# A macaron layer on one core: the second routing in two parts, rows 0 to 2 inside the last attention and row 3 inside the second FFNs

## The reference

```
x = x + 0.5 * ffn(layernorm(x))        # first FFN
x = x + attention(layernorm(x))
x = x + 0.5 * ffn(layernorm(x))        # second FFN

ffn(x):  logits = x.reshape(b, 512*512) @ switch_w.T + switch_b      # 8 experts, 8 MB of weights
         gate, idx = top_k(softmax(logits), 2)                       # per row of the batch
         o = sum over the 2 experts of gate * (gelu(xh @ w1 + b1) @ w2 + b2)   # heads of 32 features
         return (x + o) @ w3.T + b3
attention(x): q, k, v, a, g = x @ w_in.T;  q normed per head, k = tanh(k), a = clip(sigmoid(a+2))
         mem = recurrence of k*v with decay a over the tokens (chunks of 64)
         y = g*(q*mem) + (1-g)*v;  return y @ w_out.T
```

## Time and profile before

| | |
|---|---|
| median of 3 runs | 538.1 us |
| profiled execution: time, span | 537.86 us, 536.1 us |
| PE, PEld, DVE, ACT, POOL busy | 91%, 66%, 78%, 40%, 19% of the span |
| mean granted TensorE clock | 0.967 |
| read from HBM, written | 39.34 MB, 8.39 MB |
| attention of row 3 | about 351 to 407 us |
| output tiles of row 3 | 407 to 418 us |
| second routing, its choice | 418 to 431 us, 431 to 442 us |
| second FFNs of rows 1 to 3 with the W tiles of rows 0 to 3 | 456.7 to 536.1 us |

### The profile page before, as it was taken

The page is one execution under the profiler, slowest core; times in us unless marked ns, Lnnn a source line. Parts: engine busy times, 40 slices in busy tenths (PEclk is TensorE's granted clock), DMA queues, the critical chain, the costliest instruction groups (busy, mean ns, idle before and its releaser), DMA issues.

```text
span 536.1 us, 8572 instructions
## 1 busy us (share of the span) xinstructions
PE 487.3 (91%) x3184; PEld 353.8 (66%) x3204; DVE 416.6 (78%) x801; ACT 217.1 (40%) x348; POOL 103.3 (19%) x112
## 2 busy tenths in 40 slices
PE   0556999998999999999999999999999848999997
PEld 0544676666687666768766676866667725777775
DVE  3868888999776599887559988758997779878642
ACT  0226653523724222471412247242244338665640
POOL 5140036000002700001350000145111320021220
PEclk9796999999999999999999999999999968999999
DMA  8999020000102000010200001033665060131112
GB/s 338 409 376 409 3 78 2 1 1 0 40 20 74 26 1 0 2 40 21 98 0 0 0 0 39 20 137 135 240 226 223 4 208 31 41 104 54 59 56 82
DMA packets 16370, 48.19 MB, mean 90 GB/s; under 512 B 1232, under 2 KB 1232, under 8 KB 14544
## 3 DMA queue, kind: packets, MB, share of 16 engines
q1 hardware_dynamic: 16336, 47.73, 24.0%
HBM read 39.34 MB, written 8.39 MB: 89 GB/s over the span
## 4 chain that ended last, share of the span: by engine, by line
PE 73%; DVE 13%; issue 5%; SPq 3%; DMA 3%; POOL 2%; ACT 1%; POOLq 0%; DVEq 0%; ACTq 0%
PE bank L436 11%; PE bank L438 10%; PE bank L437 10%; PE bank L740 8%; PE bank L739 8%; PE bank L742 8%; DMA route_w<-in_switch_w 3%; SPq L462 2%; PE bank L611 2%; PE bank L593 2%; PE bank L703 2%; PE bank L706 2%; PE bank L711 2%; POOL rs L1146 2%; PE bank L562 2%
## 5 line engine op out<-in xcount | busy, mean ns | idle before, releaser
L739 PE MATMUL bank<-xh,win_hi 128*128 128x512 f32 x256 | 112.6, 440 | 0.0
L740 PE MATMUL bank<-xl,win_hi 128*128 128x512 f32 x256 | 100.6, 393 | 0.0
L742 PE MATMUL bank<-xbf,win_lo 128*128 128x512 bf16 x240 | 65.9, 381 | 1.0
L739 PEld LDWEIGHTS bank<-xh,win_hi 128*128 128x128 f32 x256 | 48.2, 188 | 15.9 <-DVE qn L1432 0.2
L1140 POOL TENSOR_TENSOR rstd<-mv,neg_half 128x1 f32<-128x1 f32 x16 | 9.6, 597 | 249.3 <-DVE mv L1393 249.3
L740 PEld LDWEIGHTS bank<-xl,win_hi 128*128 128x128 f32 x256 | 48.2, 188 | 10.1
L1146 POOL TENSOR_TENSOR rs<-ms,neg_half 128x16 f32<-128x16 f32 x16 | 46.6, 2934 | 23.9 <-DVE ms L1427 23.9
L436 PE MATMUL bank<-w_hi,z_hi 128*128 128x512 f32 x124 | 50.1, 404 | 0.0
L438 PE MATMUL bank<-w_hi,z_lo 128*128 128x512 f32 x124 | 48.5, 391 | 0.0
L437 PE MATMUL bank<-w_lo,z_hi 128*128 128x512 f32 x124 | 48.5, 391 | 0.0
L742 PEld LDWEIGHTS bank<-xbf,win_lo 128*128 128x128 bf16 x256 | 21.1, 98 | 30.7 <-issue 17.4
(11 more groups left out here) (216 smaller groups left out, 1057.5 us busy)
## 6 DMA issues: line engine op xcount, KB each, us to landing
route_w<-in_switch_w SPq DMA_DIRECT2D x14, 512.0 KB, 13.9
route_w<-in_switch_w SPq DMA_DIRECT2D x5, 1024.0 KB, 4.7
xa<-in_x SPq DMA_DIRECT2D x4, 1024.0 KB, 5.3
route_w<-in_switch_w SPq DMA_DIRECT2D x2, 2048.0 KB, 15.5
out<-x SPq DMA_DIRECT2D x16, 256.0 KB, 2.0
x_dram<-x1p SPq DMA_DIRECT2D x12, 256.0 KB, 2.0
xa<-x_dram SPq DMA_DIRECT2D x3, 1024.0 KB, 5.8
x_chunk<-in_x SPq DMA_DIRECT2D x2, 1024.0 KB, 17.6
```

The source lines that it names most:

```text
L739: pe.matmul(bank[:], win_hi[:, c, r, k, :], xh[:, k, :], start=(k == 0), stop=False)
L740: pe.matmul(bank[:], win_hi[:, c, r, k, :], xl[:, k, :], start=False, stop=False)
L742: mm = pe.matmul(bank[:], win_lo[:, c, r, k, :], xbf[:, k, :], start=False, stop=(k == KC - 1))
```

## The change

Row 3 is taken out of the second routing.

Rows 0 to 2. The statistics of x2 are taken on DVE when its tiles are added (`x2_stats`: two inside `row_end`, two behind it). POOL makes the factors (`x2_rstd`: two operations), ACT normalises the row in place in the next row's attention, between the second and the third square of q (`x2_norm`), and SP stores it to a second scratch tensor (`store_xn`, `xn_dram`). In the attention of row 3 SP loads chunks of three normalised rows (`chunk_load`), ACT weaves them (`weave`, three copies), SP streams the routing weights in pieces of 1 MB through a ring of three slots (`piece_load`), and PE runs the four passes behind jobs 2, 4, 6 and 8 (`route_early`) and the logits behind job 9. DVE's sums and places stand in the gap of group 2, the selection for row 0 behind group 2 and in the gap of group 3. The exponential is a power of e on POOL (`gate_exp`).

Row 3. The output tiles of row 3 are woven with the second FFN of row 0, much as in `row_end`. ACT normalises row 3 behind the first chunk of FFN B+1 (`x2_norm(B - 1, xn_c)`), and PE runs one pass behind each chunk of FFN B+1 (`route_last`), with all weights streamed a second time through a ring of four slots. Logits, places and gates of row 3 follow in FFN B+2.

The W tiles of FFN B use one PSUM bank (`o_bank[1]`), since the other holds the sums of row 3's routing. The inputs of FFNs B+1 and B+2 are loaded from `xn_dram` normalised; DVE's `normalise` of them is gone.

The core of the diff:

```diff
+        ROUTE_AFTER = {2: 0, 4: 1, 6: 2, 8: 3}
+        WEAVE_AFTER = {1: 0, 3: 1, 5: 2, 7: 3}
+        LOGITS_AFTER = 9
...
+            sp.wait_ge(s_wlo, WIN_PARTS)
+            piece_load(0, 0, ring_a)
             sp.wait_ge(s_obf, last_base)
+            piece_load(1, 1, ring_a)
+            piece_load(2, 2, ring_a)
+            store_xn(B - 2)
+            sp.wait_ge(s_xns, 16 * NT * (B - 1))
+            chunk_load(0)
+            for t in range(NT):
+                if t + 1 < NT:
+                    sp.wait_ge(s_wv, t + 1)
+                    chunk_load(t + 1)
+                sp.wait_ge(s_rm, NT + t + 1)
+                for p in range(2 * t + RING, min(2 * t + 2 + RING, PIECES)):
+                    piece_load(p, p % RING, ring_a)
...
+            def out_late(n, chunks):
+                if n == 0 and chunks[0] == 0:
+                    pe.wait_ge(s_sh, 2)
+                elif n >= 2 and chunks[0] == 0:
+                    pe.wait_ge(s_obf, job_last(f"A{n - 2}") + 1)
+                out_tile(B - 1, n, o_bank[n % 2], chunks)
+
+            for c in range(2):
+                t1(B, c, B - 1, False)
+                out_late(c, range(KC - 1))
+            t1(B, 2, B - 1, False)
+            t1(B, 3, B - 1, False)
             hidden(B, 0, B - 1)
+            for c in range(2):
+                out_late(c, range(KC - 1, KC))
             hidden(B, 1, B - 1)
-            for f in range(B, 2 * B):
+            for c in range(KC):
+                if c % 2 == 0:
+                    out_late(2 + c // 2, range(2))
+                experts_out(B, c)
+                if c >= 1:
+                    t1(B + 1, c - 1, None, True)
+                if c < 2:
+                    hidden(B, c + 2, None)
+                else:
+                    hidden(B + 1, c - 2, None)
+                if c % 2 == 0:
+                    out_late(2 + c // 2, range(2, KC))
+            for f in range(B + 1, 2 * B):
                 for c in range(KC):
...
+                    if f == B + 1:
+                        route_last(c)
...
+                    if f == B + 1 and c == 0:
+                        x2_norm(B - 1, xn_c)
...
+            hidden_lo(B, 3)
+            z_split(B, 2, x_bank[2])
+            xt_split(B + 1, 1)
+            x2_late(0)
+            x2_late(1)
+            hidden_lo(B + 1, 0)
+            out_late(3)
+            z_split(B, 3, x_bank[3])
+            xt_split(B + 1, 2)
+            x2_late(2)
+            x2_late(3)
+            hidden_lo(B + 1, 1)
```

More of the change, by code:

```diff
@@ L565, in route, with route_pass @@
                     mm.then_inc(s_rm, 1)
+            def route_pass(t, ring, width, columns):
+                per = D // HD // 2
+                for d in range(D // HD):
+                    w = ring[(2 * t + d // per) % len(ring)].rearrange("p (d e c) -> p d e c", d=per, e=E)
+                    for j in range(RT):
+                        mm = pe.matmul(o_bank[0][j * B * RC:j * B * RC + width, 0:E * RC], columns(d * HD + j * RC),
+                                       w[:, d % per, :, j * RC:(j + 1) * RC],
+                                       start=(t == 0 and d == 0), stop=(t == NT - 1 and d == D // HD - 1))
+                mm.then_inc(s_rm, 1)
@@ L721, in q_back, with in_part @@
                 mm.then_inc(s_qt, 1)
-            def in_part(b, first):
+            def in_part(b, first, after=lambda job: None):
                 for t in range(NT):
@@ L942, in y_out, with group @@
                 act.activation(y_hi[:, c, :], yt[:], ACT.Copy).then_inc(s_yh, 1)
[L944 removed]
+            def group(b, c, after=lambda job: None):
                 def bank(r):
@@ L966, in q_square, with x2_norm, weave, attention @@
                 act.activation(q_sq[t % 2][:], q_bank[t][:], ACT.Square).then_inc(s_sq, 1)
-            def attention(b, between=lambda c: None):
+            def x2_norm(b, dst):
+                act.wait_ge(s_p2, 2 * b + 2)
+                if dst is x1p:
+                    act.wait_ge(s_x2, 16 * NT * (b + 1))
+                done = s_xn2 if dst is x1p else s_x3
+                rows = dst if dst is x1p else dst[:].rearrange("p (t d) -> p t d", t=NT)
+                for t in range(NT):
+                    act.activation(rows[:, t, :], x1p[:, t, :], ACT.Identity, scale=rstd2[:, t:t + 1],
+                                   bias=shift[:, t:t + 1]).then_inc(done, 1)
+            def weave(t):
+                act.wait_ge(s_ck, 16 * (t + 1))
+                if t == 0:
+                    act.wait_ge(s_t2, NT * B)
+                else:
+                    act.wait_ge(s_rm, NT + t)
+                for b in range(B - 1):
+                    ins = act.activation(woven.rearrange("p (d b c) -> p d b c", b=B - 1, c=RC)[:, :, b, :],
+                                         x1p[:, b, :].rearrange("p (d c) -> p d c", c=RC), ACT.Copy)
+                ins.then_inc(s_wv, 1)
+            def attention(b, after=lambda job: None):
                 for t in range(NT):
                     q_square(b, t)
+                    if t == 1:
+                        x2_norm(b - 1, x1p)
                 for c in range(KC):
-                    group(b, c)
-                    between(c)
+                    group(b, c, after)
             def row_ffn(b):
@@ L1155, in _ @@
             ln_rstd(0)
-            with pool.Fori(0, B - 1) as b:
+            for t in range(NT):
+                q_rstd(0, t)
+            ln_rstd(1)
+            with pool.Fori(1, B - 1) as b:
+                x2_rstd(b - 1)
                 for t in range(NT):
@@ L1272, in gate @@
+                own.do(ve.tensor_reduce(b2_col[:, lo:hi], eq[:, lo:hi], AX.X, ALU.add))
                 own.wait(m)
@@ new lines, in _ @@
+            xt_split(B, KC - 1)
+            z_split(B, 0, x_bank[0])
+            select(1, B + 1, 0)
+            hidden_lo(B, 2)
+            out_late(2)
+            z_split(B, 1, x_bank[1])
+            xt_split(B + 1, 0)
+            select(1, B + 1, 1)
+            hidden_lo(B, 3)
[6 more added lines that the diff above has]
+            z_split(B, 3, x_bank[3])
```

572 lines of the change are left out of this document (297 added, 275 removed).

## The result

The changed kernel takes 550.9 us (median of 4 runs, 550.8 to 553.2) against 538.15 (537.9 to 538.7): ratio 1.0248, 95% interval 1.0226 to 1.0271. It is slower by 12.8 us, outside the predicted range of 535.6 to 542.8. The profiled execution took 553.2 us, its span is 551.5, so its own difference of span is 15.4 us.

What follows compares the result with a forecast made beforehand. PE was taken to bound the second FFNs; the stretch from row 3's first output tile to the first W tile could shrink. Terms 0 + 8.0 - 19.8 + 12.8 = +1.0 us gave a median of 539.0, range 535.6 to 542.8.

Steps and rivals of the forecast that it cites:

- Heads of rows 1 to 3: Start of rows 1 to 3, with added statistics, factors, normalising and stores: cost 0, with 0.2 us to spare.
- The last attention row: Four routing passes behind attention jobs plus logits, no wait for pieces: +8.0 us, between +7.5 and +13.
- the logits: One product of 24 columns on PE in the last attention row: some 0.35 us.
- rival D: Ring starves; PE waits for weights in the attention, 1 us in three passes and once for the first chunk: 543; chance 0.10.
- From the last job to the first W tile: Stretch without routing: 26.6 us of pure work plus two waits, 29.8 instead of 49.64, so -19.8 us.
- The two waits: Between last job and first W tile, PE waits for DVE: 1.6 us for yt, 1.6 ahead of the W tile.
- FFNs B+1 to B+3: Second FFNs with row 3's routing: passes 7.6, logits 0.35, wait 3.15, clock 1.7; +12.8 us, between +10 and +18.
- The wait for `xn_c`: Ahead of the first late pass, PE idles 3.15 us for ACT's normalised row 3.
- the stretch at 1.2 GHz behind it: After PE's idle time ahead of the first late pass, half clock loses 1.7 us.
- rival B: Issue gap comes with every other pass, +0.6 us on each of eight: 543.8; chance 0.07.
- rival C: Half clock follows each of the three waits once idle time reaches some 1.5 us: +3.4, 542.4; chance 0.18.
- The sum: Whole kernel: 0 + 8.0 - 19.8 + 12.8 = +1.0 us, a median of 539.0.

Runs made afterwards that it cites:

- a_again: The changed kernel with nothing altered, run again beside later ones; 549.76 us, ratio 1.0220 to the kernel before.
- e9_split: Changed kernel with late passes 2 to 4 split: 64 records behind the experts' output, 64 at the chunk's end; 548.35 us, ratio 1.0199.
- e1_stores_first: Changed kernel with SP issuing weight pieces 1 and 2 after the normalised row's stores and the first chunk load; 547.72 us, ratio 1.0175.
- e8_best: Changed kernel plus four edits: stores first, output addition before statistics, piece waits per half, late passes behind next W tile with earlier first activation; 536.01 us, ratio 0.9964.
- e10_fill: Changed kernel with 11 needless 512-column matmuls on PE in the wait for xn_c; 549.75 us, ratio 1.0212.
- e7_behind_tile: Changed kernel with late passes behind the next chunk's W tile and xn_c's first activation ahead of hidden_hi's copies; 545.36 us, ratio 1.0147.
- e2_no_later_pieces: Changed kernel without loading weight pieces 3 to 7 for the routing of rows 0 to 2; 550.17 us, ratio 1.0245.
- e11_best_sel: e8_best with the second half of the selection and its gates on DVE moved behind the last group; 541.40 us, ratio 1.0054.

## Why the prediction was wrong

**Heads of rows 1 to 3: right.** PE reaches the place of the earlier trace rows at 369.81, 369.83 before. From the transposes behind row 0's wait (136.29 now, 136.34 before) it is 233.5 us in both. Other executions reach the place between 369.2 and 370.4; in the two earliest, `a_again` and `e9_split`, the clock did not fall behind row 0's wait of 2.1 us, which lies ahead of the heads.

**The last attention row: the step that failed.** It was put as "no wait, by less than 1 us" and +8.0; it is +20.4 in the first profiled execution and +15.5 in `a_again` (52.7 - 37.2, from the place that PE reached 0.6 us earlier). What was in the sum is right: a pass took 1.92 us (1.9), four of them 7.7. What the runs put beside it, for `a_again`:
- The first chunk. PE waited 4.24 us for the weave (4.73 in the first); by the starts 4.3 are lost. The prediction gave the weave's own length its place and never followed what the chunk load waits for: stores queued behind 3 MB of pieces that the change itself issues 4 us earlier. `e1_stores_first` removes it.
- The clock behind that wait, 1.5 us: the pass takes 3.40 us instead of 1.92.
- A hand-over of about 0.28 us ahead of each pass (in `e8_best` the job's last row at 369.64 would let the next start at 370.33; the pass starts at 370.61): 1.1 us in four.
- Pieces: 0.4 us in `a_again`, 5.0 in the first execution beyond the hand-overs. The 4.7 us to land were the median of five pieces of the kernel before. Beside another piece and a chunk load the one that a pass waits for took 5.6 to 6.2 in `a_again` and 6.9 to 8.2 in the first execution; the prediction had allowed 5.5 to 5.9.
- The first set of transposes, 0.36 us, which the prediction counted in the next stretch, and the logits, 0.14 us instead of 0.35.

For the waits rival D named the mechanism, at 4 us and one chance in ten; its first-chunk part is in every profile with SP's order of the changed kernel, as waits of 4.0 to 4.7 us.

**From the last job to the first W tile: right.** 29.65 us in both executions, 30.0 with the set of transposes that stands ahead of the cut, against 29.8. The two waits are 1.16 and 2.21 instead of 1.6 and 1.6, each by the releaser named.

**FFNs B+1 to B+3: the mechanism right, two terms missing.** +15.0, or +17.2 in `a_again`, against 12.8. The wait for `xn_c` is 3.18 (3.15), the stretch at 1.2 GHz behind it cost 1.5 (1.7), the passes 1.9 each, with 0.2 of hand-overs at each (a chunk with a pass lasts 7.79 us, one without 5.68). Missing were the breaks inside two of four passes, 0.83 and 1.09 us (1.11 and 1.37 in `a_again`), rival B's term, and half clock behind the 2.2 us wait, rival C's, which came in `a_again` and not in the first execution. I had given each the whole of the remainder, as if only one of them could come true. Against rival B the prediction said that a single pass has only 128 records and that the first break came after 153. The kernel before has a second one, which the earlier trace rows don't show, after 134:

```profile
428.60 1.95 PE L562 MATMUL bank<-route_w,xn_z 128*32 128x64 f32 x122 [1.17 <-issue]
```

And a number of records counted from the start of a pass is no protection: the breaks came after 121 records of pass 2 and 92 of pass 3.

The Trainium skill (Runtime: NRT & Kernel Launch, Instruction fetch mechanics) says that crossing a block of instructions is mostly hidden. The trace agrees for PE's long matmuls, which show no break, and nearly for the passes of `e8_best` (one of 0.31 us). Passes of 128 short records behind the hidden layer lose 0.8 to 1.6 us per break, at a place that moves with the stream (`e10_fill`), and nothing in bursts of 64 (`e9_split`). If these breaks are crossings of a block, which fits but isn't shown by any releaser, the trace disagrees there.

**The sum.** 8.0 - 19.8 + 12.8 = +1.0 was forecast; 20.4 - 20.0 + 15.0 = +15.4 came in the profiled execution, and -0.6 + 15.5 - 20.0 + 17.2 = +12.1 in `a_again`, whose time is close to its kernel's median. Of the 11.1 us between 1.0 and 12.1, 5.8 are the first chunk with its clock, 1.9 the hand-overs at the eight passes, 0.4 the pieces, 2.6 the breaks by the starts and 1.6 the fall of the clock behind the W tile's wait; that is 12.3, and terms of the other sign, the earlier start of 0.6 and the logits with 0.4, make up most of the difference.

What stays open: the timed executions of a kernel with such waits spread by 2 to 8 us, those of the kernel before by 1 to 3, and a profile shows one execution. Two edits whose profiles show 1.7 us less (`e10_fill`) or 6.8 less (`e7_behind_tile`) gave 0.4 and 3.9 in the ratio to the kernel before, against `a_again`. Which of the waits for pieces or falls of the clock the other runs had can't be read. Also open is why a wait of 2.2 us was followed by half clock in some executions and not in others (so was row 0's, of 2.1 us, in 11 of the 13 profiled executions with the change), and one of 4.03 in `e2_no_later_pieces` was not.

## What to carry to other kernels

When a change adds a stream of loads, redo the landing time of everything else in the same queue, and above all of small stores that something waits for: 2.1 us became 7.4. Take a landing time from a row with as many transfers under way as the new kernel will have. A wait on PE costs twice where the clock falls behind it, and fixing one wait uncovers the next limit (here the pieces), so an edit that measures nothing alone can be worth 1.5 to 2.5 us beside another. Rivals that can all be true at once should be added, not weighed against each other.

## What the hardware showed that I had not expected

- Idle time put down to issue was two things: a wait for a DMA (it ended with a landing each time in the first execution, and is named at 389.13 in `e8_best`) and a break at a fixed place of the instruction stream.
- Beside POOL's 128x512 addition, DVE's two-input operations on 24 columns took 1.19 and 1.30 us instead of 0.24 and 0.18, while the reductions kept theirs (0.16 to 0.18 us). The Trainium skill (SBUF — State Buffer, SBUF: two separate sides) says that the two engines share a port pair as an exclusive lock, which a DVE operation with two SBUF inputs needs against a GpSimd one that reads SBUF; the rows agree.
- In the changed kernel each fall of the clock cost about the same, 1.5 to 1.7 us by the granted clock of the rows behind it. That is no constant: behind the wait of 5.04 us in `e11_best_sel` it cost 2.4, and in the kernel before the clock stayed at its lower level from 433 to 446.7, from the start of the wait of 4.31 us on, with waits of 1.17 and 1.91 us just ahead of it. In the last attention and the second FFNs of the changed kernels none came behind a wait of 1.76 us or less; of waits of 2.1 us and more some had one and some not.
